# Attention with a guarded softmax and a mixture of experts: the guard from the largest value of each channel in place of norms

## The reference

```
q, k = x @ wq.T, x @ wk.T                       # (batch, 1024, 16 heads, 16)
q_mag, k_mag = softplus(q), softplus(k)
q_embed = [q_mag * cos(pos * f), q_mag * sin(pos * f)]
k_embed = [k_mag * cos(pos * f + bias), k_mag * sin(pos * f + bias)]
scores = q_embed . k_embed / 4                  # 32 terms each
attn = softmax(scores)
```

```
key = jax.random.key(seed);  ks = jax.random.split(key, 6)
wq = normal(ks[1], (256, 256)) / 16;  wk = normal(ks[2], (256, 256)) / 16
x  = normal(jax.random.fold_in(jax.random.key(seed), 1), (4, 1024, 256))
```

## Time and profile before

| | |
|---|---|
| median of 3 runs | 1170.53 us (1170.35 to 1170.7) |
| span of the profiled execution | 1170.2 us |
| TensorE matmul busy | 975.3 us, 83% |
| VectorE | 695.9 us, 59% |
| ScalarE | 648.7 us, 55% |
| GpSimd | 444.8 us, 38% |
| mean granted TensorE clock | 0.914 of 2.4 GHz |

### The profile page before, as it was taken

The page is one execution under the profiler, slowest core; times in us unless marked ns, Lnnn a source line. Parts: engine busy times, 40 slices in busy tenths (PEclk is TensorE's granted clock), DMA queues, the critical chain, the costliest instruction groups (busy, mean ns, idle before and its releaser), DMA issues. The chain is left out here.

```text
span 1170.2 us, 15296 instructions
## 1 busy us (share of the span) xinstructions
PE 975.3 (83%) x5541; PEld 570.9 (49%) x5541; DVE 695.9 (59%) x1119; ACT 648.7 (55%) x750; POOL 444.8 (38%) x295
## 2 busy tenths in 40 slices
PE   4597999999998999998999997933378998889870
PEld 2332334444533434533444442422378898889870
DVE  7855275377485267586457642275177656775536
ACT  1276887776776776787776786900123332333224
POOL 3454054053067044048234124034144534444321
PEclk8698999999998999999999998966688988899895
DMA  5597644453646625537626438100434243342228
GB/s 194 180 256 246 155 107 166 108 143 120 154 140 225 154 71 189 115 123 212 164 72 187 107 96 202 46 23 31 160 105 109 48 117 91 105 93 44 23 29 281
DMA packets 72494, 151.85 MB, mean 130 GB/s; under 512 B 9267, under 2 KB 41204, under 8 KB 71632
## 3 DMA queue, kind: packets, MB, share of 16 engines
q1 hardware_dynamic: 52928, 101.59, 32.5%
q0 software_dynamic: 19472, 49.04, 14.7%
HBM read 88.73 MB, written 61.95 MB: 129 GB/s over the span
## 5 line engine op out<-in xcount | busy, mean ns | idle before, releaser
L527 ACT ACTIVATE prob<-spsum 128x1024 f32<-128x1024 f32 x512 | 493.2, 1021 | 177.6 <-PE spsum L665 177.4
L680 PE MATMUL opsum<-prob,val 128*17 128x512 f32 x2048 | 272.2, 603 | 11.3 <-DVE oraw L912 8.8
L665 PE MATMUL spsum<-qst,kst 97*128 97x512 f32 x512 | 157.5, 429 | 15.0 <-issue 9.7
L665 PE MATMUL spsum<-area_q,kst 97*128 97x512 f32 x512 | 156.3, 426 | 2.9 <-issue 2.8
L665 PEld LDWEIGHTS spsum<-qst,kst 97*128 97x128 f32 x512 | 87.8, 192 | 139.3 <-ACT prob L527 98.5
L665 PEld LDWEIGHTS spsum<-area_q,kst 97*128 97x128 f32 x512 | 86.4, 190 | 124.4 <-ACT prob L527 67.6
L448 POOL TENSOR_TENSOR onorm<-oraw,oden 128x512 f32<-128x512 f32 x32 | 45.4, 1418 | 257.1 <-DVE oden L919 257.0
L417 POOL TENSOR_TENSOR square<-raw 128x512 bf16<-128x512 f32 x32 | 59.9, 1871 | 163.5 <-DVE raw L766 163.4
L919 DVE RECIPROCAL oden<-oden 128x256 f32<-128x256 f32 x64 | 112.2, 1753 | 2.2
L1096 POOL DMA_INDIRECT sum_scratch<-eo,add_idx x40 | 62.1, 1553 | 131.3 <-ACT eo L1185 131.3
L1176 ACT ACTIVATE hraw<-hp,b 128x640 f32<-128x640 f32 x64 | 50.9, 796 | 87.0 <-DVE hid L1258 47.4
(11 more groups left out here) (168 smaller groups left out, 1219.0 us busy)
## 6 DMA issues: line engine op xcount, KB each, us to landing
split_scratch<-area_s POOLq DMA_DIRECT2D x56, 512.0 KB, 4.2
kst<-split_scratch SPq DMA_DIRECT2D x45, 512.0 KB, 13.5
area_k<-in_w SPq DMA_DIRECT2D x16, 1024.0 KB, 7.6
qst<-split_scratch SPq DMA_DIRECT2D x24, 512.0 KB, 7.3
area_q<-split_scratch SPq DMA_DIRECT2D x21, 512.0 KB, 7.0
dispatched<-blank POOLq DMA_DIRECT2D x1, 5300.0 KB, 27.3
rows<-dispatched SPq DMA_DIRECT2D x8, 662.5 KB, 4.4
xT<-in_xT SPq DMA_DIRECT2D x4, 1024.0 KB, 16.1
```

Source lines behind the costliest of these rows:

```text
L527: act.activation(prob[u % NPB][:], spsum[u % NSB][:].rearrange("p a n -> p (a n)"), ACT.Exp, scale=HD ** -0.5).then_inc(s_exp, 1)
L665: ins = pe.matmul(spsum[u % NSB][:, e, :], kst[par][:, j, P * kt:P * (kt + 1)], qst[par][:, j, HALF * qh:HALF * (qh + 1)], start=True, sto ...
L680: ins = pe.matmul(opsum[32 * j:32 * j + HD + 1, :], val[b % 2][:, kt, h0 + j, :], prob[(2 * s + j // 2) % NPB][:, HALF * (j % 2):HALF * (j ...
```

## The change

The guard's bound is made otherwise. The square, the norms jobs and their waits go. VectorE takes, at the end of split_unit, the largest value of each channel over the unit's tokens straight from raw; after four units it multiplies, per channel, the largest query by the largest key, and the count job becomes one matmul that adds these products over the 16 channels of each head (8 heads at a time). The largest of the 8 sums is compared with 60 x 4, and the outcome is the flag. Before, the product of two squared norms was compared with 60 x 60 x 16. What reads the flag, and what follows from it, stays as it is. The count job of a pair moves from its group's step 19 to step 18.

```
--- before.py
+++ after.py
@@ -50,15 +50,13 @@
 
     for i in range(4):
         put(-14 + 3 * i, ("qk", 0, i))
-        put(-10 + 3 * i, ("norms", 0, i))
         put(-13 + 3 * i, ("v", 0, i))
     put(-1, ("count", 0))
     for grp in range(0, NG - 2, 2):
         c, s0 = grp // 2 + 1, STEPS * grp
         for i in range(4):
             put(s0 + (1, 5, 9, 13)[i], ("qk", c, i))
-            put(s0 + (6, 10, 14, 18)[i], ("norms", c, i))
-        put(s0 + 19, ("count", c))
+        put(s0 + 18, ("count", c))
         if grp % GROUPS == 2:
             for i in range(4):
                 put(s0 + STEPS + (4, 7, 12, 15)[i], ("v", grp // GROUPS + 1, i))
@@ -146,9 +144,6 @@
         tri = sb("tri", [P, P], BF16)
         ones = sb("ones", [P, P], BF16)
         blocks_f = sb("blocks_f", [P, P])
-        blocks = sb("blocks", [P, P], BF16)
-        square = sb("square", [P, HALF], BF16)
-        ones_col = sb("ones_col", [P, 1])
         rev = sb("rev", [P, TB, EXPERTS])
         slot_base = sb("slot_base", [P, TB, EXPERTS])
         blank = sb("blank", [P, WIDE])
@@ -163,7 +158,7 @@
                  for i in range(2)]
         tops = sb("tops", [P, 4])
         top2 = sb("top2", [P, 3])
-        over = sb("over", [P, 1])
+        bound = sb("bound", [1, P // HD + 1])
         flags = sb("flags", [1, NG // 2], I32)
 
         qst = [area_q[0:ROWS + 1], sb("qst1", [ROWS + 1, GH, SEQ], F32R)[:]]
...
@@ -411,10 +406,6 @@
 
                 u = 4 * c + i
 
-                pool.wait_ge(s_raw, u + 1)
-                if u:
-                    pool.wait_ge(s_full, number["norms", (u - 1) // 4, (u - 1) % 4] + 1)
-                pool.tensor_tensor(square[:], raw[:], raw[:], ALU.mult).then_inc(s_square, 1)
                 pool.wait_ge(s_hi, u + 1)
                 pool.tensor_tensor(split[u % 2][:, 1], emb[:], split[u % 2][:, 0].bitcast(F32),
                                    ALU.subtract).then_inc(s_split, 1)
@@ -568,15 +559,12 @@
                             tok = P * (2 * i + t)
                             ins = pe.matmul(misc[:, DIM * t:DIM * (t + 1)], xT[:, k, tok:tok + P],
                                             wqkv[:, 2, k, :], start=k == 0, stop=k == KC - 1)
-                elif kind == "norms":
-
-                    pe.wait_ge(s_setup, 1)
-                    pe.wait_ge(s_square, 4 * c + i + 1)
-                    ins = pe.matmul(misc[:], blocks[:], square[:], start=True, stop=True)
                 elif kind == "count":
 
-                    pe.wait_ge(s_over, c + 1)
-                    ins = pe.matmul(misc[0:1, 0:1], over[:], ones_col[:], start=True, stop=True)
+                    pe.wait_ge(s_const, 16 * NCONST)
+                    pe.wait_ge(s_top, c + 1)
+                    ins = pe.matmul(misc[0:1, 0:P // HD], top2[:, 2:3], blocks_f[:, 0:P:HD],
+                                    start=True, stop=True)
                 elif kind == "project":
 
                     b, _, t1 = UNITS[c]
@@ -722,7 +710,6 @@
                 ins.then_inc(s, 1)
                 dve.wait_ge(s, counts[s.name])
 
-            link(dve.memset(ones_col[:], 1.0))
             link(dve.memset(opsum[:], 0.0))
 
             dve.wait_ge(s_bias, 16)
@@ -754,7 +741,6 @@
                 link(dve.memset(before[:], 0.0))
                 dve.wait_ge(s_const, 16 * NCONST)
                 link(dve.tensor_copy(tri[:], tri_f[:]))
-                tell(dve.tensor_copy(blocks[:], blocks_f[:]), s_setup)
 
             def split_unit(c, i):
 
@@ -775,6 +761,13 @@
                     v = u - 2
                     stored(dve, v // 4, v % 4)
                 tell(dve.tensor_copy(split[u % 2][:, 0], emb[:]), s_hi)
+                link(dve.tensor_reduce(tops[:, 2 * qk + half:2 * qk + half + 1], raw[:], AX.X, ALU.max))
+                if i == 3:
+
+                    for m in range(2):
+                        link(dve.tensor_tensor(top2[:, m:m + 1], tops[:, 2 * m:2 * m + 1],
+                                               tops[:, 2 * m + 1:2 * m + 2], ALU.max))
+                    tell(dve.tensor_tensor(top2[:, 2:3], top2[:, 0:1], top2[:, 1:2], ALU.mult), s_top)
 
             def read_out(job):
 
@@ -782,30 +775,16 @@
                 misc = bank(job)
                 dve.wait_ge(s_full, number[job] + 1)
                 if kind == "qk":
-                    if u := 4 * c + i:
-
-                        dve.wait_ge(s_square, u)
                     tell(dve.tensor_copy(raw[:], misc[:]), s_free)
                     tell(dve.scalar_tensor_tensor(soft[:], raw[:], -1.0, raw[:], ALU.mult, ALU.min), s_abs)
                 elif kind == "v":
                     tell(dve.tensor_copy(val[c % 2][:, 2 * i:2 * i + 2, :, 0:HD],
                                          misc[:].rearrange("p (t h d) -> p t h d", t=2, h=HEADS)), s_free)
-                elif kind == "norms":
-                    qk, half = i % 2, i // 2
-                    tell(dve.tensor_reduce(tops[:, 2 * qk + half:2 * qk + half + 1], misc[:], AX.X,
-                                           ALU.max), s_free)
-                    if i == 3:
-
-                        for m in range(2):
-                            link(dve.tensor_tensor(top2[:, m:m + 1], tops[:, 2 * m:2 * m + 1],
-                                                   tops[:, 2 * m + 1:2 * m + 2], ALU.max))
-                        link(dve.tensor_tensor(top2[:, 2:3], top2[:, 0:1], top2[:, 1:2], ALU.mult))
-                        tell(dve.tensor_scalar(over[:], top2[:, 2:3], BOUND ** 2 * HD, None, ALU.is_gt),
-                             s_over)
                 elif kind == "count":
-                    tell(dve.tensor_copy(flags[0:1, c:c + 1], misc[0:1, 0:1]), s_free)
-
-                    tell(dve.memset(top2[:, 0:1], 0.0), s_flag)
+                    link(dve.tensor_copy(bound[:, 0:P // HD], misc[0:1, 0:P // HD]))
+                    tell(dve.tensor_reduce(bound[:, P // HD:], bound[:, 0:P // HD], AX.X, ALU.max), s_free)
+                    tell(dve.tensor_scalar(flags[0:1, c:c + 1], bound[:, P // HD:], BOUND * HD ** 0.5,
+                                           None, ALU.is_gt), s_flag)
                 elif kind == "project":
                     b, t0, t1 = UNITS[c]
                     if i == 0:
```

More of the change, by code:

```diff
@@ L200, in attention @@
         s_wqk, s_trig, s_wv = sem("s_wqk"), sem("s_trig"), sem("s_wv")
-        s_setup, s_sums = sem("s_setup"), sem("s_sums")
+        s_sums = sem("s_sums")
         s_raw, s_hi = sem("s_raw"), sem("s_hi")
@@ L213, in attention @@
         s_store = [sem(f"s_store{i}") for i in range(4)]
-        s_square, s_over, s_flag = sem("s_square"), sem("s_over"), sem("s_flag")
+        s_top, s_flag = sem("s_top"), sem("s_flag")
         s_fill = [sem(f"s_fill{i}") for i in range(2)]
@@ L412, in split_rest @@
                 u = 4 * c + i
[L414 to L417, removed]
                 pool.wait_ge(s_hi, u + 1)
```

## The result

The changed kernel takes 1610.31 us (median of 4, 1604.76 to 1613.27) against 1170.44 us: a ratio of 1.376, 95% interval 1.374 to 1.378. The profiled execution has a span of 1607.9 us and a mean granted clock of 0.796. The forecast was 1610 us. The mechanism was the one foretold; the sum was right only because two of its parts were wrong by the same amount in opposite directions, which the experiments show.

What follows compares the result with a forecast made beforehand. TensorE, busy 83%, was taken to bound the kernel; 1170.5 + 448 (general path) + 9 (late start) + 1 (xT) - 7 (stall) - 7 (norms matmuls) - 4 (start) = 1610.5, so 1610 us, range 1525 to 1650.

Steps and rivals of the forecast that it cites:

- (b): Guard: flags stay zero because the chip's inputs come from another generator; only savings count, 1159.5 us; chance 0.05.
- (c): Guard: flags clear and no gain, as VectorE's longer reductions delay casts and stores, 1170 us; chance 0.02.
- The path: Attention stage, groups 0 to 3: flagged groups compute 64 score tiles each, 112 us a group, 448 for four.
- the late start: Group 0 waits for both halves of its stacks, so TensorE starts at about 64 instead of 53.8: +9 us.
- the stall: Cast at 105.76 waiting 5.4 us for a store, and TensorE with it: gone as transfers drain before group 1, -7.
- Lap: General path, one tile through the single bank misc: matmul, reduction and way back in series, 1.62 us at low clock.
- rival (a): General path: the clock stays high in the ping-pong, laps of 1.35, 1534 us; high or swinging clock had chance 0.22.
- Rival (d): General path dearer: fetched branch bodies, row transfer 6 to 7 us, laps of 1.7, xT late; about 1660 us; chance 0.11.
- leaving and resuming: Around each general path: value matmuls run alone, ACT's pipeline refills, slow laps at the low clock; 4 us a group.
- 28 norms matmuls: Attention steps: norms matmuls no longer run on TensorE, 0.24 us each, -7 us.
- Start -4: Before step 0: four norms matmuls and POOL's square go, casts shorten, with a bit of set-up less: -4 us.
- The moved reduction: VectorE's reduction goes from PSUM behind the matmul to raw behind the split: 0, at worst +6 us.

Runs made afterwards that it cites:

- clear kernel: The changed kernel with the new sums compared with 1000 instead of 240, so every flag stays zero: 1175.37 us, ratio 1.0042.
- experiment 9: The kernel before without norms matmuls and their reductions, guard left out, squares kept, chain of small products one step later: 1168.25 us, ratio 0.9942.

## Why the prediction was right, and where it wasn't

**The decision.** Right: flags set for batch 0 and nothing else. It came from the inputs, and the rows alone could not have given it; the earlier trace rows only showed that the path had never run. Rivals (b) and (c) fell with it. The clear kernel then did show no gain, as (c) had it, but by another way: the reductions were not longer. That it is the path and nothing else of the new guard was shown by setting the old guard (0.3731) and clearing the new one (1.0042).

**The path.** The forecast, with the late start, xT and the stall, was 448 + 9 + 1 - 7 = 451; measured 435, or 109 a group. It is the difference of two ratios, and their intervals leave it about 3 us either way.
- Lap: 1.62 forecast, 1.58 measured, 64 laps 101 instead of 104. The mis-sized parts are small; that it is a chain through one bank is shown by four banks (0.60 a lap).
- Clock: low, as taken; rival (a) fell in all four groups, but the high clock exists at a lap of 1.29. I had argued from one neighbouring loop, and only group 2 shows what that argument was about. Its first two laps ran at the high clock and the clock fell in the third:

```profile
360.19 0.49 PE L626 MATMUL misc<-kst,area_q 96*128 96x512 f32 x1 [1.89 <-DVE gmax L907]
...
361.47 0.72 PE L626 MATMUL misc<-kst,area_q 96*128 96x512 f32 x1 [0.78 <-DVE gmax L907]
```

Group 0 began at 0.50 after 13.9 us without work, and in groups 1 and 3 the fall lies in a wait of 6.13 and 4.47 us for VectorE after the first matmul. The Trainium skill (TensorE: Matmul & The Clock Gate, section on PSUM-queue depth-cycling) lets such loops swing between the levels; in the laps of the changed kernel there is no swing: once at 0.50, within the first three laps of a group, it stayed there to the end of the laps.
- Tail 3.2 instead of 4, the row's transfer 2.1 instead of 2.5. Rival (d) had nothing: no fetch between laps, xT waited for 0.49 us.
- Group 0: its first maxima matmul is at 61.5, not 64. The stall at 100 to 107: the store landed sooner (the cast waits 1.68 us instead of the 5.43 of the earlier trace rows), but TensorE waits 6.13 us in group 1's first lap for VectorE, which has the chain of small products and the copy before it. That is part of its 109.2, so of the 7 taken off for the stall most came back. The four groups, from the first maxima matmul to the first score matmul, make 425.5 of the 435. The other 10 hold the later start of group 0 (61.5, where the clear kernel starts its steps at about 50.3, its first exponential at 51.6 less 1.26), the vanished stall and four restarts; they were not taken apart, but for leaving and resuming there is clearly less than the 4 each that I took.

**The parts that are meant to save.** This is the step that failed. Forecast -7 - 4 = -11, measured +4.9 (ratio 1.0042). Its terms:
- 28 norms matmuls -7: right, 6.8 in experiment 9, where VectorE's reductions of them were left out too.
- Start -4: the flag's row ends at 48.25 us (L786) instead of 51.68 (L806), and the clear kernel's steps start at 50.37 instead of the 53.81 of the earlier trace rows: 3.4, right.
- The moved reduction, "which VectorE's room hides in the steps", at 0, and the maxima and the product, which moved from step 18 to 15 and have no term at all: wrong. I priced VectorE's work by its room over the stage and did not ask what stands right behind it in its queue. It is the copy that frees opsum, and TensorE waits for that. The chain at step 15 costs TensorE 2.45 to 2.64 us at four pairs and 2.1 more at the stall, and a fall of the clock behind some of these waits; moved, 12.5 of the 16 us come back. The other 3.4 were not taken apart; the count job's three waits of 2.64 us stand there now, where the forecast had "hidden at step 18".
- The bound of 2.34 for the reduction beside GpSimd was not needed: 685 to 691 ns in all 32. What is held up is the pair of one-column maxima, 1.89 us instead of 0.35 (the pair in the kernel before). The Trainium skill (SBUF — State Buffer, section "SBUF: two separate sides") says that a VectorE instruction with two inputs in SBUF and a GpSimd instruction that reads SBUF exclude each other from a shared pair of ports, for the whole instruction. The rows agree: in all 8 pairs of the clear kernel the first of the two maxima takes 1.68 to 1.86 us and ends within 0.04 us of the GpSimd remainder (459.36 and 459.35 here), the second then takes under 0.2, and the reduction with one input ran beside the same remainder unhindered.

So 451 was 16 too much and -11 was 16 too low, and 1610 is their sum: that it met the measured time to 0.3 us is luck. The range would have held either error.

## What to carry to other kernels

A guard with a slow path has to be checked against the values it will see, not against its algebra: a looser bound that is cheaper by 7 us cost 435. Work that is moved to an engine with room must be looked up in that engine's order: what stands right behind it, and who waits for that; here a chain of 2.7 us in front of one copy was dearer than the 28 matmuls that it came with. And a ping-pong through one buffer is worth more buffers even when it is rarely run: four banks took off 250 of the 435 us (two were not tried).

## What the runs showed of the hardware

- TensorE shown busy 99% of the time by the profile stayed at 1.2 GHz (granted clock 0.50) for 100 us with three matmuls in a lap of 1.58 us; with four it went to 2.4 GHz after some 6 us and kept it with laps of 1.29. Adding work made the kernel 0.041 in ratio faster.
- A VectorE instruction with two inputs of 128 x 1 numbers took 1.68 to 1.86 us where a GpSimd instruction of 2.34 to 2.38 us had started before it (8 of 8 in the clear kernel; 0.16 alone); it ended with that instruction. A reduction of 128 x 512 with one input stayed at 0.69.
- A wait of 2.5 to 2.7 us of TensorE in a stream of 2.1 us steps was followed by a stretch at half the clock in four of four places of the changed kernel (the longest 0.52 over the 7 us from 986) and in two of four of the clear one, so it can cost more than itself.
